# First attention: denominators from ones beside each head's values, outputs stored over used values, no sums of probabilities

## The reference

```python
q = layernorm(x) @ w_q                       # 16 heads of 64
k, v = split(context @ w_kv)                 # context: 8 x 1024 x 192
scores = einsum('bhqd,bhkd->bhqk', q, k) * 64 ** -0.5
attn = softmax(scores, axis=-1)
out = einsum('bhqk,bhkd->bhqd', attn, v)     # then heads joined: 8 x 512 x 1024
x = x + out @ w_out + b_out
```

## Time and profile before

| | |
|---|---|
| median of 3 runs | 3272.8 us (3272.36 to 3278.39) |
| the profiled execution | 3275.32 us, its span 3273.5 us |
| mean granted TensorE clock | 0.972 |
| first attention, about | from the start to 1901 us |
| TensorE, VectorE, ScalarE, GpSimd busy | 3103.7, 2266.9, 1631.7, 1315.2 us |

### The profile page before, as it was taken

The page is one execution under the profiler, slowest core; times in us unless marked ns, Lnnn a source line. Parts: engine busy times, 40 slices in busy tenths (PEclk is TensorE's granted clock), DMA queues, the critical chain, the costliest instruction groups (busy, mean ns, idle before and its releaser), DMA issues. The chain is left out here.

```text
span 3273.5 us, 40355 instructions
## 1 busy us (share of the span) xinstructions
PE 3103.7 (95%) x14204; PEld 1888.6 (58%) x14204; DVE 2266.9 (69%) x3673; ACT 1631.7 (50%) x1850; POOL 1315.2 (40%) x617
## 2 busy tenths in 40 slices
PE   6999999999999999999999879799999999999588
PEld 4556656556566565565565446455555555554368
DVE  5765775765766757757747434788888888887589
ACT  3453443443444434534534412376576666666288
POOL 1774774764766657757747722200000000000102
PEclk8999999999999999999999989799999999999698
DMA  8444543463453544444534232322323223322202
GB/s 232 113 112 125 129 128 101 116 162 83 116 145 90 122 126 116 112 118 119 122 106 111 65 123 64 83 50 65 68 49 72 65 49 71 69 49 56 72 13 90
DMA packets 182474, 317.40 MB, mean 97 GB/s; under 512 B 35080, under 2 KB 94288, under 8 KB 182288
## 3 DMA queue, kind: packets, MB, share of 16 engines
q1 hardware_dynamic: 182288, 315.00, 38.8%
HBM read 92.58 MB, written 29.36 MB: 37 GB/s over the span
## 5 line engine op out<-in xcount | busy, mean ns | idle before, releaser
L916 POOL TENSOR_TENSOR a_prob_sum<-a_prob_sum,a_prob 128x1024 f32<-128x1024 f32 x384 | 919.3, 2394 | 56.7 <-POOL a_prob_sum L916 2.2
L627 ACT ACTIVATE a_prob<-a_t 128x1024 f32<-128x1024 f32 x512 | 517.0, 1025 | 644.3 <-PE a_t L444 458.6
L774 DVE TENSOR_REDUCE a_mhalves<-a_m 128x1 f32<-128x512 f32 x1024 | 688.8, 680 | 105.8 <-PE a_m L408 98.3
L1669 ACT ACTIVATE a_prob<-a_t 128x1024 f32<-128x1024 f32 x512 | 497.6, 1025 | 183.9 <-PE a_t L1510 183.2
L1766 DVE TENSOR_REDUCE a_mhalves<-a_m 128x1 f32<-128x512 f32 x807 | 537.6, 685 | 61.2 <-PE a_m L1489 56.7
L451 PE MATMUL a_o<-a_prob,a_v_all 128*64 128x512 f32 x2048 | 493.7, 604 | 0.0
L408 PE MATMUL a_m<-a_kh_n,a_qz 128*128 128x512 f32 x1024 | 416.9, 419 | 7.7 <-DVE a_kl_n L768 3.4
L916 POOL TENSOR_TENSOR a_prob_sum<-a_prob 128x1024 f32<-128x1024 f32 x64 | 153.5, 2398 | 539.1 <-ACT a_prob L627 474.2
L1489 PE MATMUL a_m<-a_vh,a_qz 128*128 128x512 f32 x807 | 337.6, 438 | 9.7 <-DVE x_sb L1838 4.4
L436 PE MATMUL a_t<-a_q_hl,a_k_hh 128*128 128x512 f32 x1024 | 324.1, 398 | 0.3 <-ACT a_prob L627 0.3
L444 PE MATMUL a_t<-a_q_hm,a_k_lm 66*128 66x512 f32 x1024 | 321.3, 395 | 0.0
(11 more groups left out here) (274 smaller groups left out, 4181.5 us busy)
## 6 DMA issues: line engine op xcount, KB each, us to landing
a_k_hh<-a_kh_n SPq DMA_DIRECT2D x256, 256.0 KB, 4.3
a_k_lm<-a_kl_n SPq DMA_DIRECT2D x128, 256.0 KB, 4.8
a_q_hl<-a_qz SPq DMA_DIRECT2D x128, 128.0 KB, 2.3
a_q_hm<-a_qz SPq DMA_DIRECT2D x128, 128.0 KB, 2.4
a_q_hl<-a_ql_n SPq DMA_DIRECT2D x128, 128.0 KB, 2.3
a_vs<-a_vh SPq DMA_DIRECT2D x256, 64.0 KB, 2.3
a_wq<-wq_parts SPq DMA_DIRECT2D x63, 256.0 KB, 2.7
a_wk<-wk_parts SPq DMA_DIRECT2D x63, 256.0 KB, 2.9
```

The lines of the kernel that those rows point to most:

```text
L627: nc.scalar.activation(prob[:, t % RING], ps_t[t % 2][:, :, :], ACT.Exp, scale=SCALE0).then_inc(s_exp, 1)
L774: nc.vector.tensor_reduce(mhalves[:, qt, hd, n:n + 1], ps_m[:, n, :], AX.X, ALU.max).then_inc(s_max, 1)
L916: nc.gpsimd.tensor_tensor(acc, prob[:, (t - 1) % RING] if t == 1 else acc, prob[:, t % RING], ALU.add).then_inc(s_acc, 1)
L1669: nc.scalar.activation(prob[:, t % RB, 2 * j:2 * j + 2, :], ps_t[j][:, :, :], ACT.Exp, scale=SCALE1).then_inc(s_exp, 1)
```

## The change

The values of a pair of heads lie in `v_all` as values of head 0, 64 columns of ones, values of head 1 (`V_COLS` = 64 + 8 x 192 columns a tile). The values product of a head takes 128 columns, its values and the ones, and writes all 128 rows of a bank of its own (`ps_o[:, 0]`, `ps_o[:, 1]`): one half of the rows is the output, the other the denominator, repeated. `prob_sum`, `add_probs` and `denominators` go. ScalarE keeps output and denominators in four copies of 64 rows, after the first four exponentials of the next pair (after the last pair of a batch, at its end). The first inversion moves from before VectorE's first maximum to before its seventh and reads `den_raw`. The bank `ps_x` goes; query products and maxima rows use `ps_t[0]`. Every pair but a batch's first begins with scores. `oT` becomes a view of `v_all`'s first four tiles, so that these tiles of the next batch are projected after `project_out`. Raw weights of the start-up lie in `prob` and `v_all`. The diff, cut to its core:

```diff
-        v_all = sb("v_all", [P, KT, H0 * HD0])
+        V_COLS = HD0 + NP * 3 * HD0
+        v_all = sb("v_all", [P, KT, V_COLS])
...
-        prob_sum = sb("prob_sum", [P, 2, NQ])
         o_raw = sb("o_raw", [P, NQ])
+        den_raw = sb("den_raw", [P, NQ])
         recip = sb("recip", [P, NQ])
-        oT = sb("oT", [P, NP, NQ])
+        oT = [v_all[:, 0:QT, p * 3 * HD0:p * 3 * HD0 + P] for p in range(NP)]
...
-        ps_o = psum("o", [P, NQ])
-        ps_x = psum("x", [P, NQ])
-        out_banks = [ps_o[:], ps_x[:], ps_m[:, 0, :], ps_m[:, 1, :]]
+        ps_o = psum("o", [P, 2, NQ])
+        out_banks = [ps_o[:, 0, :], ps_o[:, 1, :], ps_m[:, 0, :], ps_m[:, 1, :]]
...
+        raw_v = prob[:, 2:4, :, :].rearrange("p c a n -> p c (a n)")
+        raw_k = v_all[:, KT - 2:KT, 0:2 * 512]
...
+        def query_bank(pr):
+            return ps_o[:, 0, :] if pr.g < 2 else ps_t[0][:, 0, :]
+        def row_bank(pr):
+            return ps_o[:, 1, :] if pr.g == 0 else ps_t[0][:, 1, :]
...
+        def values_and_ones(tile, pr, hd):
+            at = HD0 + pr.p * 3 * HD0 + hd * HD0
+            return v_all[:, tile, at:at + P]
+        def tile_of(b, i):
+            return i if b == 0 else (i + KT // 2) % KT
...
-                if pr.g != 0:
-                    pe.wait_ge(s_mkept, 2 * pr.g)
+                bank = query_bank(pr)
+                if pr.g == 1:
+                    pe.wait_ge(s_lo, 2)
+                elif pr.g != 0:
+                    pe.wait_ge(s_exp, KT * (pr.g - 1) - 1)
...
             def max_scores(pr, c):
-                if pr.g == 0:
-                    pe.wait_ge(s_lo, 2)
-                elif pr.g != 1:
-                    pe.wait_ge(s_rec, QT * (pr.g - 1))
+                else:
+                    pe.wait_ge(s_exp, KT * pr.g - 1)
                 for qt in range(QT):
-                    mm = pe.matmul(ps_x[0:HD0 + 2, qt * P:(qt + 1) * P], mcol[:, qt, :],
+                    mm = pe.matmul(row_bank(pr)[0:HD0 + 2, qt * P:(qt + 1) * P], mcol[:, qt, :],
                                    ident_r[:], start=True, stop=True)
                 mm.then_inc(s_mrow, 1)
+            def banks_read(g):
+                pe.wait_ge(s_mkept, 2 * g + 2)
+                if g + 1 < B * NP:
+                    pe.wait_ge(s_lo, 3 * (g + 1) + 2)
...
                 if t == 0:
                     pe.wait_ge(s_stk, STACKS * (pr.g + 1))
+                    banks_read(pr.g)
                 if t >= 2:
                 for hd in range(2):
-                    if t == 0:
-                        pe.wait_ge(s_mkept, 2 * pr.g + 1 + hd)
...
                 for hd in range(2):
-                    mm = pe.matmul(ps_o[hd * HD0:(hd + 1) * HD0, :],
-                                   v_all[:, t, (2 * pr.p + hd) * HD0:(2 * pr.p + hd + 1) * HD0],
+                    mm = pe.matmul(ps_o[:, hd, :], values_and_ones(t, pr, hd),
                                    prob[:, t % RING, hd, :],
                                    start=(t == 0), stop=(t == KT - 1))
                 mm.then_inc(s_pv, 1)
-            def denominators(pr, nx, nn):
-                if nn is not None:
-                    pe.wait_ge(s_lo, 3 * nn.g + 2)
-                elif nx is not None:
-                    pe.wait_ge(s_mkept, 2 * nx.g + 2)
-                else:
-                    pe.wait_ge(s_rec, QT * pr.g)
-                pe.wait_ge(s_acc, (KT - 1) * (pr.g + 2))
-                for hd in range(2):
-                    mm = pe.matmul(ps_x[hd * HD0:(hd + 1) * HD0, :], ones[:, 0:HD0],
-                                   prob_sum[:, hd, :], start=True, stop=True)
-                mm.then_inc(s_den, 1)
...
                 if pr.p == 0:
+                    pe.wait_ge(s_va, KT // 2 * (pr.g // NP + 1))
                     scores(pr, 0)
+                    pe.wait_ge(s_vd, KT // 2 * (pr.g // NP + 1))
                     scores(pr, 1)
                     if pr.g:
                         pe.wait_ge(s_x, QT * (pr.g // NP))
                     maxima(2)
-                elif pr.p == NP - 1:
+                else:
                     scores(pr, 0)
                     maxima(1)
                     scores(pr, 1, among())
                     maxima(2)
-                else:
-                    maxima(1)
-                    scores(pr, 0)
-                    maxima(1)
-                    scores(pr, 1, among())
-                    maxima(1)
...
-                pe.wait_ge(s_oraw, pr.g)
+                pe.wait_ge(s_oraw, 4 * pr.g)
...
+                t = tile_of(b, i)
+                if i >= 2:
+                    pe.wait_ge(s_va if i % 2 == 0 else s_vd, KT // 2 * b + i // 2)
...
-                    for t in range(KT):
-                        project_v(b + 1, t)
+                    banks_read(NP * (b + 1))
+                    for i in range(KT // 2):
+                        project_v(b + 1, i)
                     pe.wait_ge(s_lo, 3 * NP * (b + 1) + 6)
                 project_out(b)
                 if not last:
-                    pe.wait_ge(s_va, KT // 2 * (b + 2))
-                    pe.wait_ge(s_vd, KT // 2 * (b + 2))
+                    for i in range(KT // 2, KT):
+                        project_v(b + 1, i)
...
-                act.wait_ge(s_acc, (KT - 1) * (pr.g + 1) + (max(t - RING, 1) if t >= RING else t - RING + 1))
                 nc.scalar.activation(prob[:, t % RING], ps_t[t % 2][:, :, :], ACT.Exp,
                                      scale=SCALE0).then_inc(s_exp, 1)
...
+            first, second = slice(0, HD0), slice(HD0, P)
+            KEPT = ((den_raw[first, :], ps_o[second, 0, :]), (den_raw[second, :], ps_o[first, 1, :]),
+                    (o_raw[first, :], ps_o[first, 0, :]), (o_raw[second, :], ps_o[second, 1, :]))
+            def keep_o(g, n):
+                if n == 0:
+                    act.wait_ge(s_pv, KT * (g + 2))
+                    act.wait_ge(s_ot, g)
+                kept, bank = KEPT[n]
+                nc.scalar.copy(kept, bank).then_inc(s_oraw, 1)
             def attend(pr, nx, nn, turned=None):
                 for t in range(KT):
                     exps(pr, t)
+                    if pr.p and t < 4:
+                        keep_o(pr.g - 1, t)
...
-                keep_o(pr)
+                if pr.p == NP - 1:
+                    for n in range(4):
+                        keep_o(pr.g, n)
...
-                    dve.wait_ge(s_den, pr.g + 3)
+                    dve.wait_ge(s_oraw, 4 * pr.g + 2)
                     dve.wait_ge(s_ot, pr.g)
                 cols = slice(qt * P, (qt + 1) * P)
-                nc.vector.reciprocal(recip[:, cols], ps_x[:, cols]).then_inc(s_rec, 1)
-            INVERTED_AT = (0, 9, 11, 12)
+                nc.vector.reciprocal(recip[:, cols], den_raw[:, cols]).then_inc(s_rec, 1)
...
                 else:
                     attend(pair(b, NP - 3), pair(b, NP - 1), pair(b + 1, 0), split=b + 1)
                     attend(pair(b, NP - 2), pair(b + 1, 0), pair(b + 1, 1))
-                    keep_v(b + 1, 1)
                 for qt in range(QT):
                     invert(pair(b, NP - 1), qt)
                 if not last:
-                    for t in range(3, KT, 2):
-                        keep_v(b + 1, t)
+                    keep_v(b + 1, 1)
+                    keep_v(b + 1, 3)
                 dve.wait_ge(s_bias, b + 1)
                 for qt in range(QT):
                     dve.wait_ge(s_out, QT * b + qt + 1)
                     nc.vector.tensor_tensor(x_res[:, qt, :], out_banks[qt][:, 0:D], x_res[:, qt, :], ALU.add
                                             ).then_inc(s_x, 1)
+                if not last:
+                    keep_v(b + 1, 5)
+                    keep_v(b + 1, 7)
...
-                pool.wait_ge(s_oraw, pr.g + 1)
-                nc.gpsimd.tensor_tensor(oT[:, pr.p, :],
-                                        o_raw[:], recip[:], ALU.mult).then_inc(s_ot, 1)
-            def split_tail_low(b, sums):
-                pool.wait_ge(s_acc, sums)
+                pool.wait_ge(s_oraw, 4 * (pr.g + 1))
+                nc.gpsimd.tensor_tensor(oT[pr.p], o_raw[:].rearrange("p (t n) -> p t n", t=QT),
+                                        recip[:].rearrange("p (t n) -> p t n", t=QT), ALU.mult).then_inc(s_ot, 1)
-            def add_probs(g, split=None):
-                acc = prob_sum[:]
-                for t in range(1, KT):
...
-                    nc.gpsimd.tensor_tensor(acc, prob[:, (t - 1) % RING] if t == 1 else acc,
-                                            prob[:, t % RING], ALU.add).then_inc(s_acc, 1)
...
             def batch(b, last):
-                add_probs(b * NP)
                 if not last:
                     rstd_of(b + 1)
                 for p in range(NP - 2):
-                    add_probs(b * NP + p + 1, b + 1 if p == NP - 3 and not last else None)
+                    if p == NP - 3 and not last:
+                        split_tail_low(b + 1)
+                        pool.wait_ge(s_ctl, b + 2)
```

(40 more changed lines are left out.)

37 lines of the change are left out of this document (10 added, 27 removed).

## The result

Median of the runs after: **3629.35 us** (3627.65 to 3630.59), against 3272.97 for the kernel before on the same chip. The ratio is 1.1084, 95% interval 1.1065 to 1.1104. Forecast were 3653 us and a range of 3590 to 3715. The change costs 356 us, 24 less than forecast. The profiled execution after has a span of 3625.8 us.

What follows compares the result with a forecast made beforehand. TensorE's passes in the first attention were taken as the bound. 3275.3 + 301 (values products) + 72 (VectorE's stall) + 5 + 7 - 5 (batch ends) = 3655, less 2.5 to the median: 3653 us, range 3590 to 3715.

Steps and rivals of the forecast that it cites:

- The bound: First attention: TensorE's passes set the time, 227.7 of 229.0 us a batch; GpSimd's 1073 us of sums lie beside them.
- The values products, +4.7 per pair: TensorE's values products lose their side-by-side passes: 13.76 us added, 9.04 removed per pair, +301 us over 64 pairs.
- (c): Values products: a wide pass in a dense stream takes less, say 0.37 us; 3531 us, chance 0.03.
- (d): Values products: a wide pass goes at 0.216 us, -2.1 per pair; 3218 us, chance 0.04.
- VectorE's moved reciprocal, 1.3 x 55 = 72: Reciprocal before the seventh maximum makes TensorE stall 1.3 us at the ninth, in 55 pairs: +72 us.
- some 60 to 70 us more: Sign to look for: TensorE's waits for VectorE's reductions grow by this much, at the ninth maximum.
- ScalarE, 0: Four half copies between the next pair's first exponentials cost nothing on top; without VectorE's stall, 0.5 per pair.
- rival (a): VectorE's stall does not show, ScalarE's 0.5 per pair remains; 3609 us, chance 0.12.
- The batch's ends, +7: Batch edges: +5 for second scores awaiting a copy, +7 for pair 7's keys, -5 in the last batch.
- The two waits of the earlier trace: Last batch: TensorE's waits for GpSimd's sums, 1.90 and 4.81 us, go away: -6.7.
- Rival (b): VectorE's stall doubles to 2.6 us as late maxima start a second wait; 3725 us, chance 0.11.
- Rival (e): Values products: they stay paired, the change not doing what it says; held excluded by the text.

Runs made afterwards that it cites:

- e5: Kernel before, with GpSimd adding only one column of each head from the third tile on, denominators incomplete; 3267.41 us (0.9974).
- e9: e7 with ScalarE's four half copies moved, one ahead of the first exponential and none behind the third; 3581.23 us (1.0939).
- e2: Kernel after, with 64-column values products, both heads to rows 0 to 63 of their own banks, no denominators computed; 3706.85 us (1.132).
- e1: Kernel after, with 64-column values products, head 0 to rows 0 to 63, head 1 to rows 64 to 127, no denominators; 3271.39 us (0.9991).
- e3: Kernel after, with the old order (a maximum before the first scores) at the head of pairs 1 to 6 of a batch; 3615.57 us (1.1041).
- e7: Kernel after, with both the old order at the head of pairs 1 to 6 and reciprocals before maxima 11 to 14; 3604.98 us (1.1009).
- e4: Kernel after, with the four reciprocals moved to before maxima 11, 12, 13 and 14; 3599.28 us (1.0992).
- e10: e4 with ScalarE's four half copies placed as in e9; 3595.05 us (1.0978).
- e6: Kernel before, with the very last pair's seven additions of probabilities made by VectorE in place of GpSimd; 3268.29 us (0.9979).

## Why the prediction was right, and where a term was off

- **The bound.** Right: TensorE's passes in the first attention, 227.7 of 229.0 us. Taking 1068 us off GpSimd bought nothing in a middle pair; e5 shows it alone. Only a small reading was off: the kernel before also waits for the sums in seven other places, 0.2 us each.
- **The values products, +4.7 per pair.** Right, and it is most of the result. The wide pass starts 0.43 us after the last, as in the earlier trace rows. The middle pair without stalls, e9's, is 29.15 against 24.5: +4.65. Rivals (c) and (d), a faster wide pass, are out. The Trainium skill's page "TensorE: Matmul & The Clock Gate", section "Measured speedup vs the span model", has a figure for three column tiles; the estimate that the prediction carried over from it to two tiles made the loss of the pairing 4.4 us per pair. e2 against e1 has 6.84, both with 64 columns and the same edges, so the figure does not carry over to this case.
- **VectorE's moved reciprocal, 1.3 x 55 = 72.** The term that was mis-sized, and some 19 of the 24 us. The mechanism and its place, the ninth maximum, were right, and so was "some 60 to 70 us more" of waits (85.4 against 23.2 is 62), though they stand in two places. The size was taken from "nine maxima back to back in 6.28 us, 0.70 each", read as VectorE's own pace. It was TensorE's. Where VectorE is behind, it is quicker: the three reductions behind the reciprocal start 0.61 us apart (379.40 to 381.23, with the next reciprocal as the end). So from the first reduction to the ninth product, where the prediction has 7 x 0.70 + 0.95 and 0.2 of restart, 6.04 us, the trace has 5.53 (374.55 to 380.08): 3.99 for six reductions, 0.86 for the reciprocal, 0.68 for the seventh and the start of the product. The stalls measure 0.95 per pair: 0.60 at the ninth with its restart, and 0.35 at the fourth, which was not foreseen. There the new order puts two products side by side (the x2 at 375.51, 0.48 us apart where those before it are 0.70 apart), and the fourth has to wait for the second's reduction; the old order in e3 takes that stall away. (1.3 - 0.95) x 55 = 19 us. With all stalls gone, from the kernel after to e9, 48.1 us are gained, 0.87 x 55.
- **ScalarE, 0.** Right for the kernel after: the last copy is hidden by VectorE's stalls. The rest of the sentence, 0.5 per pair once the stall is gone, was right once both stalls were: a middle pair has 29.63 us in e7 and 29.15 in e9, 0.48. With the stall at the ninth gone alone it was not, since e4 and e10 have the same middle pair, 29.5. The state of e7 is what rival (a) needed (3605 against its 3609 us), and it did not come without an edit.
- **The batch's ends, +7.** Pair 7's wait for the low part of its keys is there, 1.29 us at 557.50 after:

```profile
557.50 0.50 PE L436 MATMUL a_m<-a_kh_n,a_qz 128*128 128x512 f32 x1 [1.29 <-DVE a_kl_n L789]
```

The interval that holds it grew 0.8 us more than a middle pair's (26.27 to 32.66, 6.39 against 5.6); forecast 1.0. The scores at a batch's start wait 0.55 us, forecast 0.7. The two waits of the earlier trace rows are gone. Not forecast: the first values product of all comes at 75.25 us in place of 79.67, 4.4 earlier (1.5 to 4.8 in the edited versions of the kernel after), and that is most of what is left of the 24. TensorE changes between 1.2 and 2.4 GHz there; its mean granted clock from 60 to 80 us (the third number from the end, columns as in the earlier trace rows) is higher after, and what raised it was not tried. Before, then after:

```profile
60.00:80.00 20.00, 17.21 (x58) 12.11 (x60) 10.82 (x17) 7.17 (x9) 5.80 (x3) 0.75 0.70 161
...
60.00:80.00 20.00, 19.24 (x66) 13.43 (x67) 10.44 (x16) 9.20 (x11) 0.00 (x0) 0.89 0.77 183
```

- **Rival (b)**, a second stall: there is a second one, but ahead of the ninth maximum and not behind it, and not at that price, 0.95 together in place of 2.6. **Rival (e)** is excluded by the timeline.

## What to carry to other kernels

Before a product is widened to take work from another engine, look at whether it now runs beside another one: here two products in different halves of the columns took the time of one, and no column count shows that, only the starts of the passes. When an engine seems to work back to back, ask who sets the pace; its own speed is in a stretch where it is behind. And of three waits in a row only the last shows: take one away, run it, and read the list of waits again before pricing the next, and place two streams' fixed points (maxima, exponentials, copies) together.

## What the runs showed of the hardware

Two f32 passes of 64 columns in different halves start together, a pair every 0.43 us; in the same half they start 0.43 us apart, as passes of 128 columns do (e1, e2, after). Going between products of 128 and of 64 columns costs about 0.3 us per group (31.43 against 30.12 us for four groups a pair, with 32 passes about 0.43 apart in both). Not expected was how much GpSimd and VectorE held each other up. VectorE's scaling of the normalised rows, before and in e5, which differ only in the length of GpSimd's additions. Before:

```profile
L817 DVE TENSOR_SCALAR a_xn<-a_xn,a_mv,a_rstd 128x256 f32<-128x256 f32 x28 | 31.8, 1135 | 0.0
```

e5:

```profile
L817 DVE TENSOR_SCALAR a_xn<-a_xn,a_mv,a_rstd 128x256 f32<-128x256 f32 x28 | 11.3, 404 | 0.0
```

1135 against 404 ns; the kernel after has 404 too. It works the other way as well. In e6, where VectorE adds while GpSimd multiplies:

```profile
1860.19 2.14 POOL L906 TENSOR_TENSOR a_oT<-a_o_raw,a_recip 128x512 f32<-128x512 f32 x1 [3.57 <-DVE a_recip L790]
1861.30 3.45 DVE L814 TENSOR_TENSOR a_prob_sum<-a_prob_sum,a_prob 128x1024 f32<-128x1024 f32 x2
```

GpSimd's product takes 2.14 us, against a mean of 1.28 in the kernel before. In the middle pairs none of it reached the time (24.5 us before and in e5), since VectorE's scaling has room beside TensorE's passes; a kernel bound by VectorE would have to look.
